# Causal scores of a linear-attention kernel: blocks of 32 keys on eight 64x32 tiles, second token half in reversed order of 32-blocks

## The chip, the cores and the metric

The kernel runs on one core of a Trainium2 chip (trn2). The metric is device time in microseconds (us), median of the runs. Before the change it is 446.14 us, with runs between 445.23 and 446.38.

## What is computed

For each of 16 sequences ("rows" of the kernel, B = 16) of T = 256 tokens and C = 128 channels, the kernel computes a layer norm, causal linear attention with 16 heads, a soft mixture of experts, and a residual. The change touches the attention only. Its part of the reference, cut:

```python
xn = layernorm(x)
q, k, v = split(xn @ Wqkv + bqkv)            # 16 heads of 8 channels
qf, kf = features(q), features(k)            # exp(clip(projection)), 64 values for each token and head
# causal linear attention, written as running sums:
kv_cur = cumsum(kf[:, f] * v[:, d]);  k_cur = cumsum(kf)
out = (qf . kv_cur) / max(qf . k_cur, 1e-6)
x = x + out @ Wout + bout + experts(xn)
```

The kernel evaluates the running sums as scores: S[key, query] = kf(key) . qf(query), masked so that a key counts only for queries at or after it, and then S times v.

## The kernel before

A row has 256 tokens in two halves of 128, one token to a partition. Within the second half the two blocks of 64 tokens stand in swapped order: partitions 0 to 63 hold tokens 0-63 and 192-255, partitions 64 to 127 hold tokens 64-127 and 128-191. `load_x` and `store` (L349 to L360) do this with two DMAs each.

Heads are worked in eight pairs p = 0 to 7. `project(b, g)` (L1093) makes the features of two pairs, `clip` on VectorE (L848) and `feature_exp` on ScalarE (L578) finish them in `feat`, where the two heads of a pair lie in partitions 0-63 and 64-127. `scores(b, p)` (L1109) forms the score blocks of both heads of one pair: for each of the four entries of `BLOCKS` (L30) and each head one f32 matmul of 64 contraction rows by 64 keys, with the queries streaming. An entry is (first key, first output partition, first query, last query, output column). The four entries stream 256, 192, 64 and 128 columns; entries one and three write partitions 0-63, two and four partitions 64-127, so each half of the output partitions gets 320 columns, and with two heads four 64x64 tiles of the array are in use. The output is `p_s` for even p and `p_t` for odd p, one PSUM bank for each head.

`evac_a` (VectorE, L854, with the mask `causal`) and `evac_b` (ScalarE, L584; the mask follows on GpSimd, L488) copy the scores to SBUF; `evac_pair` (ScalarE, L590, and L482) does both heads of pairs 6 and 7. `context` (L1127) multiplies them with v in 24 f32 matmuls on four 128x32 tiles, the line L1133. `causal` has 384 columns: 256 for keys of the first half, 128 for keys of the second.

The order on TensorE is written out by hand in `row` (L1356). Scores always come as two pairs one after the other, first on `p_s`, then on `p_t`; here each such couple is named by its pairs:

- logits of this row (L1070), scores 6 and 7 of the row before, transposed logits (L1211), context of heads of pairs 0 to 3 (L1133), shift (L1222, L1230), project 0 and 1 (L1105), slot sums (L1238), the next row's qkv product (L1070), slots transposed (L1246);
- scores 0 and 1, context of pairs 4 to 7 (L1133), scores 2 and 3;
- expert hidden layer (L1070), project 2 and 3, second expert layer (L1271, L1280) with transposes of the row before (L1175, L1181), combine (L1292), attention output (L1187), transposes of a later row (L1081);
- scores 4 and 5. Then the next row begins with its logits; rows 2 to 13 run in a hardware loop of two rows, with a branch at its end.

Before each call of `scores` the engine's sequencer waits for the exponentials (`fe_ok`) and for the bank to be free (`cl_ok` after the clip for pairs 0, 1, 4, 5; `ea_ok` and `eb_ok` after the evacuations for the others). The last entry of `BLOCKS` raises `sa_ok` and `sb_ok`, for which the evacuations wait.

Rows 0 and 15 are special: the first has its own prologue (weights are loaded, split and scaled, `causal` and `ident` are built on GpSimd from L428 on) and the last ends with a chain of small steps and the last store.

Of the kernel before, what the change touches and what calls it, by code (L numbers as in the profile page):

```python
# [13 lines left out]
B, T, C = 16, 256, 128  # L14
# [12 lines left out]
DEN_FLOOR = 1e-6  # L27
CLIP = 20.0
LOWEST = -3.0e38
BLOCKS = ((0, 0, 0, T, 0), (64, 64, 64, T, 64), (128, 0, 128, 192, 256), (192, 64, 128, T, 256))  # L30
LN_EXP = "natural_log_exp_and_others"
GELU = "gelu_and_others"
SQRT = "sqrt_and_others"
# [10 lines left out]
def landed(b, extra):  # L44

    i, u = b
    return i * 32 + 32 * extra

def after(eng, sem, value):  # L50
# [43 lines left out]
def build(nc, x, Wqkv, bqkv, Wout, bout, omega, nodes, weights, gamma_x, gamma_slot, slot_embeds,  # L94
          w1, w2, out):
    with ExitStack() as ctx:
        def sb(name, shape, dt=F32):
            return ctx.enter_context(nc.sbuf_tensor(name, shape, dt))
# [4 lines left out]
        def sem(name):  # L103
            return ctx.enter_context(nc.semaphore(name))
# [4 lines left out]
        causal = sb("causal", [128, 384])  # L109
# [34 lines left out]
        xin = sb("xin", [128, 2, TILES, C])  # L144
# [34 lines left out]
        out_sb = sb("out_sb", [128, 2, TILES, C])  # L179
# [129 lines left out]
        def heads_out(b):  # L309

            return p_t if is_row(b, B - 1) else x23

        def omega_part(t, r):

            return t[:, :, :].rearrange("p g (h r m) -> p (g h) r m", h=2, r=R)[:, :, r, :]
# [32 lines left out]
        def _(sp):  # L348
            def load_x(b, off):  # L349
                hold(sp, xg_ok, count(b, 1, -1))  # L350
                hold(sp, xr_ok, count(b, 1, -1))
                v = x[bass.ds(off, T), :].rearrange("(a p) c -> p a c", p=64)
                sp.dma_start(xin[0:64, b[1], :, :], v[:, 0:4:3, :]).then_inc(d_x[b[1]], 16)
                sp.dma_start(xin[64:128, b[1], :, :], v[:, 1:3, :]).then_inc(d_x[b[1]], 16)

            def store(b, off):
                hold(sp, o2_ok, count(b, 1, 1))
                v = out[bass.ds(off, T), :].rearrange("(a p) c -> p a c", p=64)
                sp.dma_start(v[:, 0:4:3, :], out_sb[0:64, b[1], :, :]).then_inc(d_out[b[1]], 16)
                sp.dma_start(v[:, 1:3, :], out_sb[64:128, b[1], :, :]).then_inc(d_out[b[1]], 16)  # L360

            def turn_stack(b):
                hold(sp, sthi_ok, count(b, 1, 1))
# [17 lines left out]
            first = x[0:T, :].rearrange("(a p) c -> p a c", p=64)  # L381
            sp.dma_start(xin[0:64, 0, :, :], first[:, 0:4:3, :]).then_inc(d_x[0], 16)
            for h in range(2):
                sp.dma_start(se_rows[:, 2 * h:2 * h + 2, :], slot_embeds[256 * h:256 * h + 256, :].rearrange(
                    "(c p) d -> p c d", p=128)).then_inc(d_se[h], 16)
# [12 lines left out]
            for u in range(2):  # L398
                o = 64 * u
# [4 lines left out]
            for u in range(2):  # L404
                o = 64 * u
# [10 lines left out]
            run_rows(sp, row)  # L416
            store((B // 2 - 1, 0), (B - 2) * T)
            sp.wait_ge(o2_ok, B)
            v = out[(B - 1) * T:B * T, :].rearrange("(a p) c -> p a c", p=64)
            sp.dma_start(v[:, 0:4:3, :], out_sb[0:64, 1, :, :]).then_inc(d_out[1], 16)  # L420
            for u in range(2):
                sp.wait_ge(d_out[u], 16 * B)

        LATE = 2

# [2 lines left out]
        def _(pool):  # L428
# [14 lines left out]
                                          fill=0.0, base=0, pattern=[[1, 128]], channel_multiplier=-1)  # L443
            last.then_inc(pool_id, 1)
            pool.wait_ge(pool_id, 4)
            pool.memset(causal[0:64, 320:384], 0.0).then_inc(pool_id, 1)
            pool.memset(causal[64:128, 256:320], 1.0).then_inc(pool_id, 1)
            pool.wait_ge(pool_id, 6)
            pool.tensor_scalar(neg_ident[:, :], ident[:, :], -1.0, None, ALU.mult).then_inc(pool_id, 1)
            pool.memset(xg[:, :, :, C:C + 1], 1.0)  # L450
            pool.memset(proc[:, :, C:C + 1], 1.0)
# [89 lines left out]
            v = s_sb[:, 6, 1, :].rearrange("p (a t) -> p a t", t=128)[:, 0:3:2, :]  # L541
# [5 lines left out]
        def _(act):  # L547
# [81 lines left out]
            first = x[0:T, :].rearrange("(a p) c -> p a c", p=64)  # L629
            act.dma_start(xin[64:128, 0, :, :], first[:, 1:3, :]).then_inc(d_x[0], 16)  # L630
# [133 lines left out]
            ctx_copy(last_row, 1)  # L764
            attn_copy(last_row)
            act.wait_ge(o2_ok, B)
            v = out[(B - 1) * T:B * T, :].rearrange("(a p) c -> p a c", p=64)
            act.dma_start(v[:, 1:3, :], out_sb[64:128, 1, :, :]).then_inc(d_out[1], 16)

        @block.vector
# [294 lines left out]
        def _(pe):  # L1066
# [42 lines left out]
            def scores(b, p):  # L1109
                after(pe, fe_ok, count(b, 4, p // 2 + 1))  # L1110
                if p in (0, 1, 4, 5):
                    hold(pe, cl_ok, count(b, 4, (1, 2, 0, 0, 3, 4)[p]))
                else:
                    hold(pe, ea_ok, count(b, 6, p - 1))
                    hold(pe, eb_ok, count(b, 6, p - 1))
                dst = (p_s, p_t)[p % 2]
                for keys, rows, lo, hi, o in BLOCKS:
                    for u, done in enumerate((sa_ok, sb_ok)):
                        f = feat[64 * u:64 * u + 64, p % 4, :]
                        mm = nc.tensor.matmul(dst[rows:rows + 64, u, o:o + hi - lo], f[:, T + keys:T + keys + 64],  # L1120
                                              f[:, lo:hi], start=True, stop=True, skip_group_check=True)
# [194 lines left out]
            pe.wait_ge(pool_id, 7)  # L1316

            def first_row():

# [118 lines left out]
```

## Time and profile before

| | before |
|---|---|
| median of three runs | 446.14 us (445.23 to 446.38) |
| the profiled execution | 445.07 us |
| its span, first to last instruction | 443.3 us |
| TensorE matmul busy | 431.2 us, 97% |
| VectorE busy | 347.5 us, 78% |
| ScalarE busy | 320.0 us, 72% |
| GpSimd busy | 186.3 us, 42% |
| granted TensorE clock | 0.999 of 2.4 GHz |

The page of the profile gives busy time of each engine, the span in 40 slices, and the chain of work that ended last. The trace behind it can be asked for groups of instructions (by line, tile and shape), for instructions in order of time in a stretch, and for what each engine waited for. PE is TensorE's matmuls, PEld its weight loads, DVE VectorE, ACT ScalarE, POOL GpSimd, SP SyncE; a q behind a name is the engine's sequencer or its DMA issue. An f32 matmul shows as two records of the same shape, so that a score of one pair (eight matmuls) is sixteen records.

### The profile page before, as it was taken

The page shows a single profiled execution, that of the slowest core. Times are in us where ns is not written, and L with a number is a line of the kernel's source. Part 1 is how long each engine was busy: PE and PEld are TensorE (multiplying, and loading weights), DVE is VectorE, ACT ScalarE, POOL GpSimd, SP SyncE. Part 2 cuts the span into 40 slices and gives each one's busy share as a digit, 9 for nine tenths or more (in the row PEclk, how much of TensorE's full clock was granted, in tenths as well). Part 3 has the DMA queues.
Part 4 walks back from the last instruction along what each step waited for, and adds up shares of the span by engine and source line. Part 5 has one row for each costly group of instructions (what it writes and reads, how often), then busy time and mean ns, then how long its engine had stood idle before and what let it go on. Part 6 is the DMA issues. An engine that isn't in the chain of part 4 may idle for free.

```text
span 443.3 us, 15786 instructions
## 1 busy us (share of the span) xinstructions
PE 431.2 (97%) x5726; PEld 361.1 (81%) x5726; DVE 347.5 (78%) x872; ACT 320.0 (72%) x533; POOL 186.3 (42%) x278
## 2 busy tenths in 40 slices
PE   6889999999999999999999999999999999999896
PEld 3568888888888889888888988888898888889785
DVE  7898777978878797878869787796978779576653
ACT  4767786858768686786868678586876859677681
POOL 5424444543435444343643443464345345434320
PEclk9999999999999999999999999999999999999999
DMA  4400321030202003020110302011030200203001
GB/s 93 107 25 3 62 49 27 1 63 14 53 20 47 18 6 59 12 47 24 37 23 12 59 12 47 24 22 37 12 59 12 47 12 9 51 1 61 2 1 25
DMA packets 45323, 14.37 MB, mean 32 GB/s; under 512 B 35376, under 2 KB 45168, under 8 KB 45296
## 3 DMA queue, kind: packets, MB, share of 16 engines
q1 hardware_dynamic: 44448, 13.48, 14.8%
q10 hardware_dynamic: 720, 0.53, 0.4%
q8 instruction: 17, 0.28, 0.3%
q0 software_dynamic: 128, 0.01, 0.1%
q14 instruction: 10, 0.08, 0.1%
HBM read 3.44 MB, written 2.10 MB: 12 GB/s over the span
## 4 chain that ended last, share of the span: by engine, by line
PE 93%; DVE 4%; ACT 2%; issue 1%; DVEq 0%; ACTq 0%
PE x L1070 20%; PE p_s L1120 10%; PE p_t L1120 8%; PE x L1271 7%; PE x L1238 7%; PE x L1280 6%; PE x L1292 6%; PE x L1133 5%; PE p_s L1133 5%; PE x L1211 4%; PE p_s L1105 2%; PE x L1222 2%; PE x L1246 2%; PE x L1187 2%; PE p_t L1105 2%; PE x L1175 1%
## 5 line engine op out<-in xcount | busy, mean ns | idle before, releaser
L488 POOL TENSOR_TENSOR s_sb<-s_sb,causal 128x256 f32<-128x256 f32 x96 | 68.3, 731 | 79.5 <-ACT s_sb L584 79.5
L578 ACT ACTIVATE feat<-arg,f_bias 128x1024 f32<-128x1024 f32 x64 | 71.8, 1147 | 8.4 <-DVE arg L848 8.3
L848 DVE TENSOR_SCALAR arg<-p_s,f_low,f_high 128x1024 f32<-128x1024 f32 x32 | 42.9, 1340 | 18.7 <-PE p_s L1105 12.2
L1120 PEld LDWEIGHTS p_s<-feat 64*64 64x64 f32 x1024 | 38.8, 132 | 17.2 <-issue 15.5
L1120 PE MATMUL p_s<-feat 64*64 64x256 f32 (+3 forms) x1024 | 49.5, 309 | 1.3 <-ACT feat L578 1.3
L329 POOL TENSOR_TENSOR qk_sq<-qkv 128x512 f32<-128x512 f32 x15 | 15.6, 1040 | 82.9 <-DVE qkv L825 82.9
L482 POOL TENSOR_TENSOR s_sb<-s_sb,causal 128x512 f32<-128x512 f32 x30 | 37.6, 1276 | 26.0 <-ACT s_sb L590 26.0
L1120 PE MATMUL p_t<-feat 64*64 64x256 f32 (+3 forms) x1024 | 47.1, 299 | 0.3 <-issue 0.3
L1120 PEld LDWEIGHTS p_t<-feat 64*64 64x64 f32 x1024 | 41.3, 133 | 1.8 <-issue 0.4
L848 DVE TENSOR_SCALAR arg<-p_t,f_low,f_high 128x1024 f32<-128x1024 f32 x32 | 42.7, 1335 | 0.0
L1238 PEld LDWEIGHTS x<-xg,disp 128*128 128x128 f32 x256 | 29.9, 191 | 8.2 <-ACT disp L606 8.2
L1271 PEld LDWEIGHTS x<-w_sb,hid_t 128*128 128x128 f32 x256 | 29.9, 191 | 7.1 <-ACT hid_t L618 6.6
L584 ACT ACTIVATE s_sb<-p_s 128x384 f32<-128x384 f32 x48 | 23.5, 490 | 15.8 <-PE p_s L1120 15.8
L889 DVE TENSOR_REDUCE maxima<-x 128x2 bf16<-128x512 f32 x32 | 20.6, 686 | 17.0 <-PE x L1211 17.0
L1238 PE MATMUL x<-xg,disp 128*128 128x129 f32 x256 | 33.0, 281 | 0.7 <-ACT disp L606 0.5
L1271 PE MATMUL x<-w_sb,hid_t 128*128 128x128 f32 x256 | 33.1, 282 | 0.1
L618 ACT ACTIVATE hid_t<-x 128x1024 f32<-128x1024 f32 x32 | 32.7, 1021 | 0.3
L590 ACT ACTIVATE s_sb<-p_s 128x768 f32<-128x768 f32 x15 | 12.2, 812 | 28.1 <-PE p_s L1120 28.1
L1292 PE MATMUL x<-proc,comb_t 128*128 128x129 f32 x256 | 31.5, 275 | 0.0
L1280 PE MATMUL x<-w_sb,hid_t 128*128 128x128 f32 x256 | 31.2, 275 | 0.0
L1292 PEld LDWEIGHTS x<-proc,comb_t 128*128 128x128 f32 x256 | 29.9, 191 | 0.2 <-issue 0.2
L1280 PEld LDWEIGHTS x<-w_sb,hid_t 128*128 128x128 f32 x256 | 29.8, 192 | 0.0
(165 smaller groups left out, 1035.4 us busy)
## 6 DMA issues: line engine op xcount, KB each, us to landing
xin<-in_L_attn_x_dram SPq DMA_DIRECT2D x31, 64.0 KB, 2.3
out_dram<-out_sb SPq DMA_DIRECT2D x31, 64.0 KB, 2.1
se_rows<-n_L_ffn_slot_embeds_dram SPq DMA_DIRECT2D x2, 128.0 KB, 4.4
w_f<-in_L_ffn_w_dram SPq DMA_DIRECT2D x1, 256.0 KB, 4.0
w_sb<-in_L_ffn_w_dram SPq DMA_DIRECT2D x1, 256.0 KB, 4.0
stack_t<-stack SPq DMA_TRANSPOSE x16, 4.3
wqkv_f<-in_L_attn_Wqkv_dram ACTq DMA_DIRECT2D x1, 192.0 KB, 4.1
bqkv_bc<-in_L_attn_bqkv_dram ACTq DMA_DIRECT2D x1, 192.0 KB, 4.8
```

Source lines behind the costliest of these rows:

```text
L482: pool.tensor_tensor(v, v, m, ALU.mult).then_inc(mb_ok, 1)
L488: pool.tensor_tensor(v, v, m, ALU.mult).then_inc(mb_ok, 1)
L578: nc.scalar.activation(feat[:, k:k + 2, :], arg[:, k:k + 2, :], ACT.Exp, bias=f_bias[:, 0:1]).then_inc(fe_ok, 1)
L618: nc.scalar.activation(hid_t[:, 2 * half:2 * half + 2, :], (x01, x23)[half][:, :, :], ACT.Gelu).then_inc(ge_ok, 1)
L848: nc.vector.tensor_scalar(arg[:, k:k + 2, :], (p_s, p_t)[g % 2][:, :, :], f_low[:, 0:1], f_high[:, 0:1], ALU.max, ALU.min).then_inc(cl_ok, 1)
L1070: mm = nc.tensor.matmul(dst, a, w, start=start and i == 0, stop=stop and i == 2, skip_group_check=True)
L1120: mm = nc.tensor.matmul(dst[rows:rows + 64, u, o:o + hi - lo], f[:, T + keys:T + keys + 64], f[:, lo:hi], start=True, stop=True, skip_grou ...
L1133: mm = nc.tensor.matmul(dst[32 * q:32 * q + 32, j, :], vw[:, b[1], kt, QUADS * a + q, :], s_sb[:, p, q % 2, o:o + 128], start=(kt == 0 and ...
L1238: mm = nc.tensor.matmul(x01[:, half, 129 * (c % 2):129 * (c % 2) + 129], disp[:, j, 128 * c:128 * c + 128], xg[:, b[1], j, :], start=(j == ...
L1271: nc.tensor.matmul(x01[:, c // 2, o:o + 128], hid_t[:, m, 128 * c:128 * c + 128], w2_sb[:, m, :], start=(m == 0 and c % 2 == 0), stop=Fals ...
L1280: mm = nc.tensor.matmul(x01[:, c // 2, o:o + 128], hid_t[:, m, 128 * c:128 * c + 128], w2_sb[:, m, :], start=False, stop=(m == 3), skip_gr ...
L1292: mm = nc.tensor.matmul(x23[:, 0, 129 * j:129 * j + 129], comb_t[:, c, 128 * j:128 * j + 128], proc[:, c, :], start=(c == 0 and j == 0), s ...
```

## The change

`BLOCKS` gets eight entries of 32 keys instead of four of 64. For keys k = 0, 32, 64, 96 of the first half the queries k to 255 stream (256, 224, 192 and 160 columns), written to output partitions k to k+31. The second half of the tokens is now stored in reversed order of its four blocks of 32: position block 4 holds tokens 224-255, block 7 holds tokens 128-159. There the block of keys at 128+k meets the positions 128 to 128+k+31: 32, 64, 96 and 128 columns. Each of the four groups of 32 output partitions gets 288 columns, and with two heads eight 64x32 tiles are in use. Loads and stores of a row take four DMAs of 32 partitions each, instead of two of 64; the mask is set with six small memsets instead of two; counts in semaphores follow. The first load and the last store are split between SyncE and ScalarE, two DMAs each instead of one.

```diff
-BLOCKS = ((0, 0, 0, T, 0), (64, 64, 64, T, 64), (128, 0, 128, 192, 256), (192, 64, 128, T, 256))
+KEYS = 32
+BLOCKS = (tuple((k, k, k, T, k) for k in range(0, 128, KEYS))
+          + tuple((128 + k, k, 128, 128 + k + KEYS, 256) for k in range(0, 128, KEYS)))
@@ landed
-    return i * 32 + 32 * extra
+    return i * 64 + 64 * extra
@@
+        def quarter(rows, q):
+
+            v = rows.rearrange("(a p) c -> p a c", p=32)
+            return v[:, q:8 - q:7 - 2 * q, :]
@@ load_x (store likewise, with out and out_sb)
-                v = x[bass.ds(off, T), :].rearrange("(a p) c -> p a c", p=64)
-                sp.dma_start(xin[0:64, b[1], :, :], v[:, 0:4:3, :]).then_inc(d_x[b[1]], 16)
-                sp.dma_start(xin[64:128, b[1], :, :], v[:, 1:3, :]).then_inc(d_x[b[1]], 16)
+                for q in range(4):
+                    sp.dma_start(xin[32 * q:32 * q + 32, b[1], :, :], quarter(x[bass.ds(off, T), :], q)
+                                 ).then_inc(d_x[b[1]], 16)
@@ first load on SyncE (ScalarE takes q = 2, 3), and the last store in the same way
-            sp.dma_start(xin[0:64, 0, :, :], first[:, 0:4:3, :]).then_inc(d_x[0], 16)
+            for q in range(2):
+                sp.dma_start(xin[32 * q:32 * q + 32, 0, :, :], quarter(x[0:T, :], q)).then_inc(d_x[0], 16)
@@ causal
-            pool.memset(causal[0:64, 320:384], 0.0).then_inc(pool_id, 1)
-            pool.memset(causal[64:128, 256:320], 1.0).then_inc(pool_id, 1)
-            pool.wait_ge(pool_id, 6)
+            for q in range(4):
+                if q > 0:
+                    pool.memset(causal[32 * q:32 * q + 32, 256:256 + 32 * q], 1.0).then_inc(pool_id, 1)
+                if q < 3:
+                    pool.memset(causal[32 * q:32 * q + 32, 288 + 32 * q:384], 0.0).then_inc(pool_id, 1)
+            pool.wait_ge(pool_id, 10)
@@ scores
-                        mm = nc.tensor.matmul(dst[rows:rows + 64, u, o:o + hi - lo], f[:, T + keys:T + keys + 64],
+                        mm = nc.tensor.matmul(dst[rows:rows + KEYS, u, o:o + hi - lo], f[:, T + keys:T + keys + KEYS],
                                               f[:, lo:hi], start=True, stop=True, skip_group_check=True)
-                        if keys == 192:
+                        if keys == T - KEYS:
                             mm.then_inc(done, 1)
```

## Rows read from the trace of the kernel before

**Rows 1.** The page: busy time and share of the span by engine; clock by slice.

```profile
PE 431.2 (97%) x5726; PEld 361.1 (81%) x5726; DVE 347.5 (78%) x872; ACT 320.0 (72%) x533; POOL 186.3 (42%) x278
...
PEclk9999999999999999999999999999999999999999
...
PE 93%; DVE 4%; ACT 2%; issue 1%; DVEq 0%; ACTq 0%
```

**Rows 2.** Windows of one row each: stretch, its length, busy time of each engine.

```profile
core 0: us, PE busy (x) PEld busy (x) DVE busy (x) ACT busy (x) POOL busy (x), PEclk, DMA share, GB/s
...
199.00:225.20 26.20, 26.20 (x358) 22.30 (x357) 21.41 (x54) 19.60 (x33) 11.59 (x17) 1.00 0.15 30
225.20:251.40 26.20, 26.16 (x358) 22.20 (x357) 21.26 (x54) 19.37 (x32) 11.32 (x17) 1.00 0.15 30
```

**Rows 3.** Groups by shape, stretch 211.55 to 212.9: xcount | busy us, mean ns.

```profile
L1120 PE MATMUL p_t<-feat 64*64 64x256 f32 x4 | 0.6, 377 | 0.0
...
L1120 PE MATMUL p_t<-feat 64*64 64x192 f32 x4 | 0.5, 322 | 0.0
...
L1120 PE MATMUL p_t<-feat 64*64 64x128 f32 x4 | 0.4, 269 | 0.0
...
L1120 PE MATMUL p_t<-feat 64*64 64x64 f32 x4 | 0.3, 217 | 0.0
```

**Rows 4.** Groups of weight loads by shape, stretch 210.1 to 213.0.

```profile
L1133 PEld LDWEIGHTS x<-s_sb,vw 128*32 128x32 f32 x48 | 1.2, 110 | 0.1
L1120 PEld LDWEIGHTS p_t<-feat 64*64 64x64 f32 x16 | 0.6, 134 | 0.0
```

**Rows 5.** Line L1120 in the 0.02 us from 211.60: engine op xcount: duration ns min/median/max.

```profile
L1120 PEld LDWEIGHTS p_s<-feat x3: 129/129/129, 211.6 to 211.6; 64*64 64x64 f32 x3
L1120 PE MATMUL p_s<-feat x3: 373/427/427, 211.6 to 211.6; 64*64 64x256 f32 x2, 64*64 64x192 f32 x1
```

**Rows 6.** Line L1120 on PE from 212.00 to 212.05: what is in flight.

```profile
L1120 PE MATMUL p_s<-feat x8: 269/350/427, 211.6 to 212.0; 64*64 64x256 f32 x4, 64*64 64x192 f32 x2, 64*64 64x128 f32 x2
```

**Rows 7.** PE in order of time: start us, us, what; scores 2 and 3.

```profile
210.15 1.52 PE L1133 MATMUL x<-s_sb,vw 128*32 128x128 f32 x48
211.60 0.77 PE L1120 MATMUL p_s<-feat 64*64 64x256 f32 x16
212.20 0.72 PE L1120 MATMUL p_t<-feat 64*64 64x256 f32 x16
212.85 0.50 PE L1070 MATMUL x<-slot_hi,w_hi 128*128 128x512 f32 x1
```

**Rows 8.** The same for scores 0 and 1 and the clip before them on DVE.

```profile
207.97 1.33 DVE L848 TENSOR_SCALAR arg<-p_t,f_low,f_high 128x1024 f32<-128x1024 f32 x1
...
208.80 0.77 PE L1120 MATMUL p_s<-feat 64*64 64x256 f32 x16
209.45 0.77 PE L1120 MATMUL p_t<-feat 64*64 64x256 f32 x16
```

**Rows 9.** ACT and PE in order of time, where the second expert layer begins.

```profile
213.94 1.28 ACT L735 ACT_TABLE_LOAD   x1
215.23 1.02 ACT L618 ACTIVATE hid_t<-x 128x1024 f32<-128x1024 f32 x1
...
216.38 2.05 PE L1271 MATMUL x<-w_sb,hid_t 128*128 128x128 f32 x16
```

**Rows 10.** DVE and PE in order of time at the end of a row.

```profile
223.78 0.42 DVE L816 TENSOR_TENSOR xt_lo<-x,xt_hi 128x256 fp32r<-128x256 f32 x1 [0.27 <-ACT xt_hi L561]
...
224.50 0.50 PE L1070 MATMUL x<-se_hi,xt_hi 128*128 128x512 f32 x1
```

**Rows 11.** Chain of waits, one piece: start us, us, what.

```profile
210.21 1.46 PE x L1133 x48
```

**Rows 12.** DMA issues of SyncE and ScalarE: start us, us; and the first norm on DVE.

```profile
0.82 0.74 SPq L382 DMA_DIRECT2D xin<-in_L_attn_x_dram  x1
4.01 2.88 SPq L324 DMA_DIRECT2D omega_f<-in_L_attn_omega_dram  x8
...
440.53 0.70 ACTq L768 DMA_DIRECT2D out_dram<-out_sb  x1
...
3.95 0.42 DVE L786 BATCH_NORM_STATS2 bn<-xin 128x6 f32<-128x128 f32 x2
```

**Rows 13.** Waits: who waited for whom, us in total, times, longest.

```profile
POOL xres L463 <- DMA bout_bc<-in_L_attn_bout_dram: 5.2, 1, 5.2
...
SPq L62 <- ACT stack L571: 166.4, 15, 16.9
```

More of the change, by code:

```diff
@@ L351, in load_x @@
                 hold(sp, xr_ok, count(b, 1, -1))
-                v = x[bass.ds(off, T), :].rearrange("(a p) c -> p a c", p=64)
-                sp.dma_start(xin[0:64, b[1], :, :], v[:, 0:4:3, :]).then_inc(d_x[b[1]], 16)
-                sp.dma_start(xin[64:128, b[1], :, :], v[:, 1:3, :]).then_inc(d_x[b[1]], 16)
+                for q in range(4):
+                    sp.dma_start(xin[32 * q:32 * q + 32, b[1], :, :], quarter(x[bass.ds(off, T), :], q)
+                                 ).then_inc(d_x[b[1]], 16)
             def store(b, off):
                 hold(sp, o2_ok, count(b, 1, 1))
-                v = out[bass.ds(off, T), :].rearrange("(a p) c -> p a c", p=64)
-                sp.dma_start(v[:, 0:4:3, :], out_sb[0:64, b[1], :, :]).then_inc(d_out[b[1]], 16)
-                sp.dma_start(v[:, 1:3, :], out_sb[64:128, b[1], :, :]).then_inc(d_out[b[1]], 16)
+                for q in range(4):
+                    sp.dma_start(quarter(out[bass.ds(off, T), :], q), out_sb[32 * q:32 * q + 32, b[1], :, :]
+                                 ).then_inc(d_out[b[1]], 16)
             def turn_stack(b):
@@ L379, in spread @@
                 return sp.dma_start(dst[:, :], src.rearrange("(a n) -> a n", a=1).broadcast_to([dst.shape[0], n]))
-            first = x[0:T, :].rearrange("(a p) c -> p a c", p=64)
-            sp.dma_start(xin[0:64, 0, :, :], first[:, 0:4:3, :]).then_inc(d_x[0], 16)
+            for q in range(2):
+                sp.dma_start(xin[32 * q:32 * q + 32, 0, :, :], quarter(x[0:T, :], q)).then_inc(d_x[0], 16)
             for h in range(2):
@@ L418, in _ @@
             sp.wait_ge(o2_ok, B)
-            v = out[(B - 1) * T:B * T, :].rearrange("(a p) c -> p a c", p=64)
-            sp.dma_start(v[:, 0:4:3, :], out_sb[0:64, 1, :, :]).then_inc(d_out[1], 16)
+            for q in range(2):
+                sp.dma_start(quarter(out[(B - 1) * T:B * T, :], q), out_sb[32 * q:32 * q + 32, 1, :, :]
+                             ).then_inc(d_out[1], 16)
             for u in range(2):
-                sp.wait_ge(d_out[u], 16 * B)
+                sp.wait_ge(d_out[u], 32 * B)
         LATE = 2
@@ L445, in _ @@
             pool.wait_ge(pool_id, 4)
-            pool.memset(causal[0:64, 320:384], 0.0).then_inc(pool_id, 1)
-            pool.memset(causal[64:128, 256:320], 1.0).then_inc(pool_id, 1)
-            pool.wait_ge(pool_id, 6)
+            for q in range(4):
+                if q > 0:
[3 more added lines that the diff above has]
+            pool.wait_ge(pool_id, 10)
             pool.tensor_scalar(neg_ident[:, :], ident[:, :], -1.0, None, ALU.mult).then_inc(pool_id, 1)
@@ L627, in spread @@
                 return act.dma_start(dst[:, :], src.rearrange("(a n) -> a n", a=1).broadcast_to([dst.shape[0], n]))
-            first = x[0:T, :].rearrange("(a p) c -> p a c", p=64)
-            act.dma_start(xin[64:128, 0, :, :], first[:, 1:3, :]).then_inc(d_x[0], 16)
+            for q in range(2, 4):
+                act.dma_start(xin[32 * q:32 * q + 32, 0, :, :], quarter(x[0:T, :], q)).then_inc(d_x[0], 16)
             spread(node_b, nodes, R).then_inc(d_feat, 16)
@@ L766, in _ @@
             act.wait_ge(o2_ok, B)
-            v = out[(B - 1) * T:B * T, :].rearrange("(a p) c -> p a c", p=64)
-            act.dma_start(v[:, 1:3, :], out_sb[64:128, 1, :, :]).then_inc(d_out[1], 16)
+            for q in range(2, 4):
+                act.dma_start(quarter(out[(B - 1) * T:B * T, :], q), out_sb[32 * q:32 * q + 32, 1, :, :]
+                              ).then_inc(d_out[1], 16)
         @block.vector
@@ L1315, in _ @@
             pe.wait_ge(vz_const, 2)
-            pe.wait_ge(pool_id, 7)
+            pe.wait_ge(pool_id, 11)
             def first_row():
```

## The prediction, made before the changed kernel was run

> **What bounds the kernel now.** I read the page first: TensorE matmuls are busy for 97% of the span, at full clock in all slices, and 93% of the chain that ended last is theirs [rows 1]. The question is whether other engines end some wait inside a row. The windows of single rows say no: of 26.20 us, TensorE is busy 26.20 and 26.16, while VectorE has 21.4 and ScalarE 19.6 [rows 2]. So a nanosecond saved on TensorE counts until another engine's line of work becomes the later one, and that I check at each place by instructions in order of time.
>
> **What a score costs now.** A row has four couples of scores, 64 in all over 16 rows. In scores 2 and 3 the first begins at 211.60, the second at 212.20, the next stage at 212.85: 1.25 us for a couple [rows 7]. By shape, 64 columns more take 322-269 = 53 ns, and 377-322 = 55: 0.83 ns for a column of a record [rows 3]. Each strip of 64 output partitions streams 320 columns in two records each: 2 x 320 x 0.83 = 531 ns. Two scores make 1.06 us of the 1.25; the remaining 0.19 are the first weight load that nothing hides, the staggered start, and the drain and change of tile shape at the end, about 0.2 between the last context matmul and the first score as well. So the score is bound by columns, not by instructions: the loads after the first are hidden.
>
> **The change, part by part.**
>
> Columns: 288 in place of 320, 2 x 288 x 0.83 = 478 ns, 53 less for a score, 106 for a couple [rows 3].
>
> The unhidden first load: 32 columns wide instead of 64. Loads of the two widths take 110 and 134 ns as records, so 24 less, once a couple [rows 4]. The staggered start: three of the four tiles begin within 0.02 us, some 6.7 ns apart [rows 5]; eight tiles need four steps more, +27 ns, once a couple. The two cancel.
>
> Sixteen matmuls in place of eight for a score, 32 records instead of 16. No row shows what eight tiles do together; the trace has four 64x64 tiles and four 128x32 tiles. From below, the cost is nothing: tiles start apart by 6.7 ns [rows 5], 32 of them are 214 ns of a score's 478. I exclude a gain. From above, the only long run of narrow tiles is the context, 48 records in 1.46 us, 30 ns each [rows 11]; 32 x 30 = 973 ns for a score. I take nothing, since 128 columns on four tiles need 4 x 0.83 x 128 / 4 = 106 ns for a round of four, 27 ns each, so that the context too is bound by its columns and not by its count.
>
> Work order inside a score: matmuls of different tiles pass one another. At 212.00 to 212.05 the 128-column records are in flight while no 64-column record is, although these stand before them in the list [rows 6]. The new lists need this over a longer stretch. I take it that each tile is served by itself; what happens if not is a rival below.
>
> Now where the 0.10 us of each couple goes. Scores 0 and 1: the second can't begin before its bank is clipped. The clip ends at 207.97+1.33 = 209.30 and the score begins at 209.45 [rows 8], 0.65 after the first instead of 0.60. Here only the second score gains: 0.05. Scores 2 and 3: 0.10. Both stand on a stretch whose other line (clip, qkv bias, norms on VectorE, then square root, evacuation, table load and GELU on ScalarE) contains no score that it waits for long. It ends at 215.23+1.02 = 216.25, and TensorE takes it at 216.38 [rows 9]. With about 0.05 for the hand-over TensorE can be earlier by 0.1 at most, so the two couples together bring 0.10, not 0.15. Scores 4 and 5: the low half of the transposed rows ends at 223.78+0.42 = 224.20, the logits begin at 224.50 [rows 10]; 0.10 fits. In the six loop ends the branch and the waits of the next row stand behind twice as many instructions in TensorE's sequencer; the trace doesn't show its lead, so between 0.10 gained and 0.10 lost, and I take nothing gained there. Scores 6 and 7: 0.10.
>
> A row gives 0.30, or 0.20 at a loop end: 9 x 0.30 + 6 x 0.20 = 3.9 us. Row 0 waits for others for much of its time and counts as nothing.
>
> DMAs. In the loop, SyncE issues four more a row, each at most 0.74 us [rows 12]; it waits 166 us for ScalarE's stacks [rows 13], and the transpose queued behind has more slack than that. Nothing. At the start, the second halves are issued behind the first ones: 0.36 us for each of the small omega issues, 0.74 for the full one [rows 12], so about 0.5 later. The first norm begins at 3.95, after a memset, so most of it is hidden: +0.1, between 0 and +0.5, as every later load moves back too. At the end nothing hides the second issue on either queue: +0.5, between 0.36 and 0.7 [rows 12]. The four more memsets on GpSimd lie ahead of a wait of 5.2 us for a DMA [rows 13]: nothing; without that cover they would cost under 1 us once.
>
> Sum: -3.9 + 0.1 + 0.5 = -3.3 us. The profiled execution took 445.07 us (span 443.3) and would take 441.8. It lies 1.1 us under the median of 446.14; against the median the forecast is 442.8 us. About 0.3% (1.3 us) is what a measurement can tell from no change.
>
> **Rivals.**
>
> (1) Slower, because the work let into the array is bounded in program order. Before, a score has eight matmuls, two for each tile, and all eight may be in flight. Suppose eight is what fits, and that the ninth enters when the first is done. The first is now also the longest: 256 columns, 2 x 213 + 27 for its load = 0.45 us. The 160-column tile is done after 2 x 133 + 27 = 0.29 and stands idle; its 128-column matmul then runs from 0.47 to 0.71, and the second score ends at 1.25 in the same way. With the drain, a couple takes 1.34 instead of 1.25: +0.09 x 64 = 5.8 us, and with the ends +0.6, less what scores 0 and 1 hide behind the clip, 451.5 us, between 448 and 454. It decides as soon as fewer than some twelve matmuls fit. For it: nothing in the trace has more than two matmuls waiting on one tile. Against it: the passing seen in rows 6, which it allows too.
>
> (2) No change: the gain of the stream is given back between the two scores of a couple. There the sequencer takes two or three waits before it may send the next sixteen matmuls. Today this hides behind 0.6 us of stream; with twice the instructions ahead and a shorter stream, a gap of up to 0.1 in scores 2-3, 4-5 and 6-7 takes all of it: 446 us, between 444.8 and 447.3.
>
> (3) Far slower: a floor on record starts of 30 ns, the context's rate [rows 11]. A score takes 32 x 30 = 0.97, a couple 2.04 with its 0.1 of drain instead of 1.25: +0.79 x 64 = 50 us, 496 us. Against it are the three starts in 0.02 us [rows 5] and the reckoning of the context's columns above. The Trainium skill speaks for a rule of this kind: "TensorEngine Tiling (Array Packing)", section Instruction Overhead, puts about 60 cycles on each matmul and advises against taking the tiling factor from a dimension that is already small, and "TensorE: Matmul & The Clock Gate", section Back-to-back issue gap, states a floor near 25 ns between starts. By that figure a score would be an estimated 0.8 us and the kernel some 28 us slower, 474 us; the starts in rows 5 disagree for different tiles.
>
> **How the numbers follow.** Forecast (column bound, 442.8) 0.52, own range 441.0 to 444.8: all 64 couples at 0.10 with nothing at the start would even be 440.2, the sequencer bounds against it give 445. Rival 1 0.27, rival 2 0.13, rival 3 0.08. The range 441.0 to 453.5 leaves out rival 3 and the outer ends of the others. Faster by over 0.3%: 0.52. Within: 0.12. Slower: 0.36.
>
> **What would show it.** Right: score couples of 1.15 us from first score to next stage, p_s to p_t about 0.55 (0.65 in scores 0 and 1), rows of 25.9 to 26.0 us. Rival 1: records of the 128-column blocks start 0.45 or later after the score's first instead of 0.3, couples of 1.3. Rival 2: first records of p_t start late, behind an idle stretch put down to issue. Rival 3: starts evenly spaced by 25 to 30 ns. The prediction is wrong at the root if the change of shape costs more with eight tiles than the 0.2 us seen, or if the evacuations start late because the last block ends last.

## The result, and the profile after

| | before | after |
|---|---|---|
| median of four runs each, on the same chip | 445.98 us (445.23 to 446.38) | 474.75 us (474.07 to 475.83) |
| span of the profiled execution | 443.3 us | 473.2 us |
| TensorE matmul busy | 431.2 us | 443.9 us |
| mean granted TensorE clock | 0.999 | 0.982 |

The changed kernel takes 1.066 times as long, with a 95% interval of 1.0645 to 1.0677. That is slower by 28.8 us, where the forecast was 3.3 us faster. It also lies far above the range of 441.0 to 453.5.

Lines of the page of after: those that correspond to [rows 1], between them the queue that carries code, and last the logits as a group of instructions:

```profile
PE 443.9 (94%) x7774; PEld 367.8 (78%) x7774; DVE 345.8 (73%) x872; ACT 320.4 (68%) x533; POOL 187.2 (40%) x282
...
PEclk9999999999899998999989999899998999999999
...
q8 instruction: 68, 1.11, 1.0%
...
PE 89%; issue 5%; DVE 4%; ACT 1%; ACTq 0%; DVEq 0%
...
L1082 PE MATMUL x<-se_hi,xt_hi 128*128 128x512 f32 x32 | 14.2, 443 | 18.2 <-issue 17.5
```

Four things differ from before. TensorE's share of the chain fell from 93% to 89%, and "issue", time in which nothing that the profile shows was waited for, rose from 1% to 5%. The clock row has five dips at equal distances. The queue that carries code (kind "instruction") moved 68 packets of 16 KB. In the page of before the same line reads:

```profile
q8 instruction: 17, 0.28, 0.3%
```

And of 18.2 us of idle time ahead of the logits, 17.5 are "issue": the logits open a row, and right before them stands the branch of the loop.

The windows around the first turn of the loop in after (stretch, its length, busy time by engine, granted clock, DMA share, GB/s):

```profile
119.00:121.00 2.00, 2.00 (x71) 1.64 (x69) 1.62 (x6) 1.56 (x3) 0.00 (x0) 1.00 0.00 0
121.00:124.00 3.00, 0.05 (x4) 0.00 (x0) 0.84 (x2) 0.54 (x2) 1.41 (x2) 1.00 0.12 28
124.00:126.00 2.00, 1.64 (x6) 1.05 (x6) 0.64 (x2) 0.00 (x0) 0.00 (x0) 0.89 0.17 39
126.00:129.00 3.00, 3.00 (x68) 2.49 (x68) 0.76 (x4) 1.10 (x2) 0.32 (x1) 0.51 0.00 0
129.00:132.00 3.00, 3.00 (x67) 2.56 (x66) 2.44 (x8) 1.13 (x3) 2.89 (x3) 1.00 0.02 5
```

From 121 to 124 all engines run dry; then TensorE works on, at first at full clock, and from 125.6 for 3.4 us at half. What it does at the turn itself is one line of the loop's own instructions, first in after, then in before (duration in ns, min/median/max; PEldq is TensorE's sequencer):

```profile
L89 PEldq COMPARE_BRANCH  x6: 82/3425/3832, 120.6 to 410.1; - x6
```

```profile
L87 PEldq COMPARE_BRANCH  x6: 76/210/251, 119.4 to 380.5; - x6
```

The branch is met six times and taken five times (the shortest, 82 and 76 ns, is the last one, which falls through). Taken, it costs 0.21 us before and 3.3 to 3.8 us after. From the start of one scores 4-5 to the next, a row without the turn takes 26.39 us in after and one with it 31.3 to 31.8: 4.9 to 5.4 us a turn, 25.6 us of the 29.9 by which the span grew.

The rest is inside the rows. PE in order of time in after, scores 6-7, read as in [rows 7]:

```profile
211.73 0.72 PE L1132 MATMUL p_s<-feat 64*32 64x256 f32 x32
212.25 0.91 PE L1132 MATMUL p_t<-feat 64*32 64x256 f32 x32
213.09 0.33 PE L1223 MATMUL x<-ident,log_sb 128*128 128x128 f32 x1
```

The first score takes 0.52, a little less than the 0.55 of the forecast, but the second takes 0.84: the couple 1.35 instead of 1.25. All four couples of a row read 1.35 at full clock, where before only scores 0 and 1 did, behind the clip [rows 8]; 3 x 0.10 a row are some 5 us. So there are two losses, and the experiments take them one by one.

### The profile page after: what moved, and what is told of

Its sections match the earlier page's. It is cut to its first block, busy times and chain, and to the rows that moved or that the text cites. A ratio compares the mean times of both kernels' runs of the same rounds, so it can differ in the third digit from the quotient of the medians.

```text
span 473.2 us, 20052 instructions
## 1 busy us (share of the span) xinstructions
PE 443.9 (94%) x7774; PEld 367.8 (78%) x7774; DVE 345.8 (73%) x872; ACT 320.4 (68%) x533; POOL 187.2 (40%) x282
## 3 DMA queue, kind: packets, MB, share of 16 engines
q8 instruction: 68, 1.11, 1.0%
## 4 chain that ended last, share of the span: by engine, by line
PE 89%; issue 5%; DVE 4%; ACT 1%; ACTq 0%; DVEq 0%
PE x L1082 19%; PE p_t L1132 10%; PE p_s L1132 9%; PE x L1283 7%; PE x L1250 7%; PE x L1292 6%; PE x L1304 6%; PE p_s L1145 5%; PE x L1145 5%; PE x L1223 4%; PE p_s L1117 2%; PE x L1234 2%; PE x L1258 2%; PE x L1199 1%; PE p_t L1117 1%
## 5 line engine op out<-in xcount | busy, mean ns | idle before, releaser
L1132 PE MATMUL p_t<-feat 64*32 64x32 f32 (+7 forms) x2048 | 58.4, 300 | 0.3 <-issue 0.3
L1132 PEld LDWEIGHTS p_s<-feat 64*32 64x32 f32 x2048 | 37.5, 110 | 18.7 <-issue 16.8
L1132 PE MATMUL p_s<-feat 64*32 64x256 f32 (+7 forms) x2048 | 48.6, 301 | 1.5 <-ACT feat L589 1.3
L1132 PEld LDWEIGHTS p_t<-feat 64*32 64x32 f32 x2048 | 45.7, 110 | 2.3 <-issue 0.4
L894 DVE TENSOR_SCALAR_CACHE_REDUCE log_sb<-x 128x512 f32<-128x512 f32 x32 | 22.1, 691 | 21.6 <-PE x L1082 21.4
L1250 PEld LDWEIGHTS x<-xg,disp 128*128 128x128 f32 x256 | 29.9, 191 | 8.1 <-ACT disp L617 8.1
L1283 PEld LDWEIGHTS x<-w_sb,hid_t 128*128 128x128 f32 x256 | 29.9, 191 | 7.1 <-ACT hid_t L629 6.6
L1082 PE MATMUL x<-se_hi,xt_hi 128*128 128x512 f32 x32 | 14.2, 443 | 18.2 <-issue 17.5
```

Source lines behind the costliest of these rows:

```text
L1082: mm = nc.tensor.matmul(dst, a, w, start=start and i == 0, stop=stop and i == 2, skip_group_check=True)
L1132: mm = nc.tensor.matmul(dst[rows:rows + KEYS, u, o:o + hi - lo], f[:, T + keys:T + keys + KEYS], f[:, lo:hi], start=True, stop=True, skip_ ...
L1250: mm = nc.tensor.matmul(x01[:, half, 129 * (c % 2):129 * (c % 2) + 129], disp[:, j, 128 * c:128 * c + 128], xg[:, b[1], j, :], start=(j == ...
L1283: nc.tensor.matmul(x01[:, c // 2, o:o + 128], hid_t[:, m, 128 * c:128 * c + 128], w2_sb[:, m, :], start=(m == 0 and c % 2 == 0), stop=Fals ...
```

## The experiments

### The loop written out, in both kernels

```diff
-    with eng.Fori(1, B // 2 - 1) as i:
+    for i in range(1, B // 2 - 1):
         for u in range(2):
             row((i, u), False, True, True)
```

> The changed kernel with rows 2 to 13 written out instead of a hardware loop (no branch on any engine; nothing else differs). Theory A (the branch at the loop's end must wait for TensorE's code to be loaded again, since a body of 2037 instructions is no longer held; five turns of some 4.8 us with the half-clock stretch behind each): the five stalls go, the 16 KB code transfers stay but lie beside the work, full clock throughout, 474.7 - 24 = 450.5 us, with couples still at 1.35. Rival B (the stall belongs to a wait or a transfer at the end of the second row, with four loads and four stores a row on SyncE): stalls of 3 us stay at the ends of rows 3, 5, 7, 9, 11, and the time stays at 470 to 475 us.

> The kernel before, written out in the same way, as control. Theory A: its branch takes 0.21 us behind a full queue and no code is loaded in its loop, so nothing is to be gained: 446 us, ratio 0.998 to 1.002. If written-out code had a price of its own (code streaming in all the time), this shows it, and the other run is to be read against this one.

Measured: the changed kernel written out 451.16 us (450.19 to 451.39), ratio to before 1.012 (1.0102 to 1.0139); the kernel before written out 444.83 us, ratio 0.9988 (0.9979 to 0.9998). The five stalls and all clock dips are gone, though now more code is streamed in than in the kernel before. The page of the changed kernel written out:

```profile
PE 436.6 (97%) x7774; PEld 362.5 (81%) x7774; DVE 345.5 (77%) x872; ACT 320.8 (71%) x533; POOL 187.1 (42%) x282
...
PEclk9999999999999999999999999999999999999999
...
q8 instruction: 62, 1.02, 0.9%
...
PE 93%; DVE 4%; ACT 1%; issue 1%; DVEq 0%; ACTq 0%
```

So writing out takes away 474.75 - 451.16 = 23.6 us, and rival B falls: waits, DMAs and matmuls are the same in both. That is a little less than the 25.6 us of the five turns, because three rows of the written-out kernel are 0.3 to 0.5 us longer than the others, 1.3 us in all; the kernel before, written out, has no such row. What is left, 451.16 - 444.83 = 6.3 us, are mostly the couples: a row takes 26.39 us against 26.02, and the 15 rows from the first scores on give 15 x 0.37 = 5.6. In the profiled executions, whose spans are 6.8 us apart, the rest are those three rows, less 0.2 us at the end of the kernel.

### Token order and DMAs without the small blocks

```diff
-BLOCKS = (eight entries of 32 keys)
+WIDE = ((64, 0, 0, 0, T, 0), (64, 64, 64, 64, T, 64), (64, 128, 0, 128, 192, 256), (64, 192, 64, 128, T, 256))
```

> The changed kernel (reversed order of 32-blocks in memory, four loads and stores a row, its mask and memsets), but with scores again in four blocks of 64 keys on 64x64 tiles, which this token order allows too. Theory: everything lost lies in the 32-key matmuls and their number; order and DMAs cost at most the first load and last store, 446.1 to 447 us, couples 1.25, no stall at the loop's end. Rival B: the stalls stay, 465 us or more.

Measured: 444.86 us (444.73 to 445.66), ratio 0.9986 (0.9977 to 0.9996); couples 1.25, 17 code packets. Nothing of the loss lies in the order of tokens, in the doubled DMAs, or in the mask. The time even lies under the 446.1 us from which I expected it, and 0.5 us under the 445.38 of the kernel before; 0.2 us of that are the end of the kernel (below).

### How large the loop's body may be

The records of TensorE's instructions from one branch to the next are 1525 before and 2037 after: 16 scores an iteration with eight f32 matmuls more each, and four records (two loads, two matmuls) for each. A kernel with eight different lists had 1925 and stalled too. Two kernels in between use 64-key blocks in some couples, 32-key blocks in the others, in the better order that is found below:

```diff
+    if 4 * b[1] + p // 2 not in (1, 2, 6):        # five_couples: (1, 2, 3, 5, 6)
+        return both(WIDE)
+    return both((SECOND + FIRST, FIRST + SECOND)[p % 2])
```

> Loop kept; the 32-key blocks (short first, then long first) only in scores 2-3 and 4-5 of even rows and 4-5 of odd rows, the last ones right before the branch; elsewhere 64-key blocks. Loop body 1717 instructions instead of 1525 (before: branch 0.21 us, no code loaded) and 2037 (changed: branch 3.3 to 3.8 us, nine 16 KB transfers a turn). Theory A1 (what counts is how many 16 KB blocks of 256 instructions the body spans; room for seven of them besides the one loaded ahead, so that the limit is near 1792): branch 0.2 us, no transfers. Theory A2 (eight-tile matmuls right before the branch bring the stall): branch over 3 us.

> The same with five of eight couples, body 1845 instructions; the look at eight lists had 1925 and stalled (3.5 to 3.9 us). Theory A1 with room for seven blocks: it stalls, over 3 us and eight or nine transfers a turn. With room for eight blocks and a favourable start of the body it may not; then the limit lies between 1845 and 1925.

Measured, one run each: 445.28 us with three couples, 472.89 with five. The branch in the first, the branch in the second, and the second's clock:

```profile
L103 PEldq COMPARE_BRANCH  x6: 76/208/234, 119.5 to 381.0; - x6
```

```profile
L103 PEldq COMPARE_BRANCH  x6: 83/3688/3848, 120.2 to 408.9; - x6
```

```profile
PEclk9999999999899998999979999799997999999999
```

Theory A2 falls, for the kernel with three couples has eight-tile matmuls right before its branch; A1 holds. Up to 1717 records the code stays with the engine from turn to turn; at 1845 nine transfers of 16 KB come in every turn, as in after, and the whole gain of a shorter stream is gone many times over. A turn costs even more here, 5.6 to 6.6 us, and in three of the five the clock stays at half for 6.8 us instead of 3.4. A later kernel had 1781 and didn't stall, so the limit lies between 1781 and 1845 records. That kernel and the one with five couples have the same number of TensorE instructions in all (7006 matmul records each), so the length of the whole program isn't what decides. The Trainium skill has the rule, which I had not weighed: "Runtime: NRT & Kernel Launch", section Instruction fetch mechanics, gives TensorE room for 2048 instructions, filled in blocks of 256, and says that a taken branch whose target is outside the current window of two pages stalls for a fetch. The traces agree with the stall and with blocks of 16 KB (68 packets, 1.11 MB). They differ in two points: a body of up to 1781 records, about seven such blocks, was kept whole and didn't stall, and the limit met here is lower than 2048 by 200 to 270 records.

The kernel with three couples shows a small loss too, at every turn, at which 1.0 us instead of 0.65 pass from p_t to the logits:

```profile
223.19 0.72 PE L1147 MATMUL p_s<-feat 64*32 64x32 f32 x32
223.71 0.72 PE L1147 MATMUL p_t<-feat 64*32 64x256 f32 x32
224.69 0.49 PE L1096 MATMUL x<-se_hi,xt_hi 128*128 128x512 f32 x1 [0.26 <-issue]
```

The branch and the next row's waits come after p_t's 64 instructions, and p_t is over before the sequencer is through with them. In the changed kernel it can't be told apart from the stall.

### Why the second score of a couple is late

In after, the first score's 128-column blocks are under way at 0.34 us, while the 256-column ones still run (TensorE, stretch 212.06 to 212.085; 18 records in flight or begun, the shortest, 269 ns, of 128 columns):

```profile
L1132 PE MATMUL p_s<-feat x18: 269/347/400, 211.7 to 212.1; 64*32 64x256 f32 x4, 64*32 64x224 f32 x4, 64*32 64x192 f32 x4, 64*32 64x160 f32 x4
```

So passing works, as in [rows 6], and rival 1 in its stated form, a window of eight, is out. But of the second score only one record has begun by 0.63 us after the first score's start; the next starts 135 ns after it, and then all follow 16.7 ns apart (stretch 212.25 to 212.37):

```profile
L1132 PE MATMUL p_t<-feat x1: 379/379/379, 212.2 to 212.2; 64*32 64x256 f32 x1
```

Two kernels with up to eight different lists of blocks each were to tell what this depends on; the list was chosen by couple and parity of the row. The second of them is written out and leaves some blocks out.

> Eight lists of blocks in one kernel, one for each couple and parity of row; the output is the same. Read: each couple's time from first score to next stage. Even rows: scores 0-1 the list of the changed kernel (control, 1.35), 2-3 all blocks of one head and then of the other, 4-5 both halves of the list reversed (160, 192, 224, 256, then 128, 96, 64, 32 columns), 6-7 the four short blocks first. Odd rows: 0-1 four 64-key blocks (control, 1.25 or 1.35 behind the clip), 2-3 the 256-column block cut in two (18 matmuls a score), 4-5 two 64-key blocks and four of 32, 6-7 four of 32 and two of 64. In the changed kernel the second score's first matmul starts in time, its second one only 92 ns after the last of the first score has streamed, as after a change of tile shape. Theory C (a score fills a limit of 16 matmuls, and what comes behind waits until all is done): any list of 16 keeps 1.35; the matmul that is late is the second with 16, and an earlier one with 18 (the last of the first score itself); lists of 12 have no such wait, unless the change between 64x64 and 64x32 tiles drains by itself. Theory D (the wait is between particular tiles, by place and order): the list by heads or the reversed one comes to 1.15 to 1.25.

> Written out, eight cases again. Two of them leave work out: scores 4-5 of even rows lack the 32-column block (14 matmuls a score), scores 2-3 of odd rows the 32- and the 64-column block (12 a score), otherwise in the order of the changed kernel. Theory W (16 places, freed in order): the late matmul of the second score is its second one with 16 a score (seen), so the fourth one with 14 and the sixth with 12; those before it start in time. Theory T (a drain before the second matmul on eight tiles, whatever the number): it is the second one in all three. Of the orders of 16: short first, then long first (scores 0-1 and 2-3 of even rows) 1.15 to 1.20 by theory W, 0-1 not under 1.2 as the clip gates it; long first, then short first (6-7 even) 1.3 or more; the same with all lists reversed (0-1 odd) 1.2; reversed long-then-short and then the changed kernel's order (4-5 odd) 1.25 to 1.3; short first in both (6-7 odd) 1.26 as in the look before.

Measured, one run each: 493.83 us for the first, which has the loop and its stalls (1925 records), and 447.16 us for the second. The couples from first score to next stage (PE in order of time; rows behind a turn or with a gap put down to issue are left out, but for the last line):

| list, first score then second | columns in the order sent | couple, us |
|---|---|---|
| as changed | 256, 224, 192, 160, 32, 64, 96, 128, both scores | 1.353 |
| one head, then the other | the same | 1.43 to 1.68 |
| reversed | 160, 192, 224, 256, 128, 96, 64, 32, both | 1.30 |
| reversed, then as changed | | 1.29 |
| long first, then short first | | 1.353 |
| as changed, 14 matmuls; 12 matmuls | less the 32; less the 32 and 64 | 1.32; 1.29 |
| short first | 32, 64, 96, 128, 256, 224, 192, 160, both | 1.26 |
| short first, then long first | | 1.170, 1.26 behind the clip |
| the same, all lists reversed | | 1.26 behind the clip |
| 64-key blocks | | 1.248, 1.35 behind the clip |
| 64-key and 32-key blocks in one score | | 1.86 to 1.97 |
| 18 matmuls a score | | 1.38 and 1.39 in the rows outside the loop; 1.82 to 2.61 in it |

The decisive rows are the two lists that leave work out. With 14 matmuls a score, the second score's third one begins in time and its fourth is late; with 12, the fifth begins in time and the sixth is late. The records of p_t that have begun by 0.64 us, with 14 (three, from three matmuls; the fourth begins at 0.65), and with 12 (seven: five matmuls, and the second records of two; the sixth begins at 0.65):

```profile
L1155 PE MATMUL p_t<-feat x3: 349/376/376, 92.9 to 93.0; 64*32 64x256 f32 x2, 64*32 64x224 f32 x1
```

```profile
L1155 PE MATMUL p_t<-feat x7: 323/349/376, 160.7 to 160.9; 64*32 64x224 f32 x4, 64*32 64x256 f32 x2, 64*32 64x192 f32 x1
```

16 + 1, 14 + 3, 12 + 5: it is always the 18th matmul from the start of the couple that is late. Theory T falls and W holds: TensorE has room for 16 f32 matmuls. The 17th gets its place when the oldest is done (in the changed kernel the 256-column one, at 0.45 us by the reckoning of the prediction), and the 18th, after this standstill, much later, although the two oldest start, and so end, only 7 ns apart: in after the weights of the 17th begin to load at 0.49 us and those of the 18th at 0.65, 160 ns behind. The list with 18 matmuls a score shows it within one score: its 17th begins at 0.35 us and its 18th, of the same shape on another tile, at 0.44, where the last two of a list of 16 begin 7 ns apart, at 0.34. That costs the couple some 0.03 us. In the loop the same couples are longer: the second score begins 0.1 us later and then has a stretch of 0.1 to 0.9 us in which no matmul starts. The cause of that is open. Where the oldest eight are the short blocks, it is the 10th matmul of the second score that is late (at 0.72 us, 1.26 in all). Where the short ones are the oldest in the first score and the long ones come first in the second, the late places fall where long blocks stream, and nothing is idle. Why the second place comes so late, no run tells; nor whether the room is counted in matmuls or in instructions, as every matmul of a score is f32. The Trainium skill gives TensorE a queue of 64 ("Advanced Engine Details and Errata", section Engine Queue Depths: 64, complicated with tiling); with four instructions for an f32 matmul the 16 seen here are the same number.

Of the expectations for the first kernel, both theories fell as they were worded. Theory C wanted 1.35 for every list of 16, and the reversed one took 1.30 and the one with short blocks first 1.26; theory D wanted 1.15 to 1.25 for the list by heads or the reversed one. Theory W is C with one thing changed: a place is given back when the oldest is done, and not when all are. Its expectations for the second kernel held, but for the reversed twin of the best list behind the clip, which took 1.26 where I expected 1.2. That blocks of both sizes in one score cost 0.6 to 0.7 us a couple more was expected only as a possibility: at every change between 64x64 and 64x32 tiles the array is emptied, and the next record begins 93 ns after the last column of the other shape (reckoned with 0.83 ns a column).

### The better order

```diff
+    return both((SECOND + FIRST, FIRST + SECOND)[p % 2])
```

> The changed kernel written out (451.2 us), with one thing more: the first score of each couple lists its short second-half blocks first (32, 64, 96, 128, then 256, 224, 192, 160 columns), the second score the long ones first (256, 224, 192, 160, then 32, 64, 96, 128). Theory W (TensorE takes 16 f32 matmuls ahead, 64 instructions, and gives a place back only when the oldest of them is done; in the changed kernel the oldest is the 256-column one, done at 0.45 us, and from standstill the second place comes some 155 ns after the first): with this order the first score's oldest eight are done by 0.32 us, so the second score's eight long ones are in time, and its short ones are sent while the long ones stream. Couples 1.15 to 1.20 instead of 1.35, 64 of them less what the clip and the GELU line hold back: 438 to 443 us. Theory T (a drain between scores on eight tiles, whatever the order): couples stay at 1.26 to 1.35, 447 to 451 us.

Measured: 443.71 us (443.43 to 445.24), ratio 0.996 (0.9947 to 0.9974): 7.4 us faster than the same kernel in the old order. The two ran on different chips, on which the kernel before took 445.57 and 445.38 us. Its couples, and how many records of p_t have begun by 0.64 us (eight, where the old order has one):

```profile
211.45 0.72 PE L1145 MATMUL p_s<-feat 64*32 64x32 f32 x32
211.97 0.72 PE L1145 MATMUL p_t<-feat 64*32 64x256 f32 x32
212.62 0.50 PE L1094 MATMUL x<-slot_hi,w_hi 128*128 128x512 f32 x1
```

```profile
L1145 PE MATMUL p_t<-feat x8: 296/335/376, 212.0 to 212.0; 64*32 64x256 f32 x2, 64*32 64x224 f32 x2, 64*32 64x192 f32 x2, 64*32 64x160 f32 x2
```

The couple takes 1.17 us: nearly the column reckoning of the prediction (1.15), now that the matmuls come in time, and theory T falls. But the time lies 0.7 us above the 438 to 443 that I expected, for two reasons. A row takes 25.84 us against 26.02 in the kernel before written out: 0.18 less, not 0.30. A little is lost because a couple gains 0.08 us and not 0.10; most of the loss is at one place, the second expert layer. In the kernel before written out, and then in this one:

```profile
214.55 1.03 ACT L618 ACTIVATE hid_t<-x 128x1024 f32<-128x1024 f32 x1
215.66 0.52 PEld L1271 LDWEIGHTS x<-w_sb,hid_t 128*128 128x128 f32 x4 [0.42 <-ACT hid_t L618]
```

```profile
215.18 1.02 ACT L641 ACTIVATE hid_t<-x 128x1024 f32<-128x1024 f32 x1
216.26 0.86 PEld L1296 LDWEIGHTS x<-w_sb,hid_t 128*128 128x128 f32 x7 [0.52 <-ACT hid_t L641]
```

Counted from the start of scores 6-7 of the row before, TensorE is 0.20 earlier at the expert layer's first product and 0.10 earlier at the second: the weight loads' wait for GELU grows from 0.42 to 0.52 us.

The second reason: written out, five rows have a gap and are 0.2 to 1.1 us longer than the others, 2.7 us in all in the profiled execution, which at 445.24 us was the slowest of the five. A transfer of code lies within a few us of each gap, but one of 16 KB comes every 7 us, so that these traces don't show that the transfers make the gaps. One of the largest, inside a score:

```profile
237.81 0.60 PE L1145 MATMUL p_t<-feat 64*32 64x256 f32 x14
239.01 0.65 PE L1145 MATMUL p_t<-feat 64*32 64x160 f32 x18 [0.60 <-issue]
```

### A version inside the limit, and one with less code

> Loop kept; in it the 32-key blocks (short first, then long first) in four of the eight couples: scores 2-3, 4-5 and 6-7 of even rows and 2-3 of odd rows; the others, among them those right before the branch, with 64-key blocks. The four rows outside the loop have 32-key blocks everywhere. Without stall: four couples of 1.17 instead of 1.25, 6 x 0.32 = 1.9 us and some 1.2 in the rows outside, so 442.5 to 444.5 us; with stalls 466 or more.

> The fastest so far (written out, short first then long first, 443.7 us), but with 64-key blocks in scores 0 and 1, where the second score waits for the clip. 64 instructions a row less to load. In the written-out kernel stretches of 0.2 to 1.0 us appear in which TensorE has nothing to do right beside a code transfer, in some rows and not in others (about 3 us in all). If they come from the rate at which code is used, they become fewer with fewer instructions; against that stand the 0.09 us by which this couple is shorter. Fewer stalls win: 441 to 443.5 us; otherwise 444 to 445 us.

Measured: 443.21 us (442.53 to 443.81), ratio 0.9948 (0.9932 to 0.9964), for the loop with four couples; 443.23 us (442.39 to 445.09), ratio 0.9951 (0.9934 to 0.9968), for the written-out one with 64-key blocks at the clip. In the first, the branch is that of the kernel before, and none of its 22 code transfers lies between the first turn and the last:

```profile
L103 PEldq COMPARE_BRANCH  x6: 76/208/239, 119.1 to 378.6; - x6
```

```profile
q8 instruction: 22, 0.36, 0.3%
```

From its second turn on two of its rows take 51.90 us, without gaps, where two rows in the loop of the kernel before take 52.22: the 0.32 that was expected. The second still has gaps, 0.1 to 0.5 us of idle time at four places. Both beat the kernel before by half a per cent; they can't be told from one another, nor for certain from the 443.71 above, so that fewer instructions aren't shown to bring fewer gaps.

## Why the prediction was wrong, step by step

**What bounds the kernel, and the columns: right.** TensorE was the bound; 288 columns take nearly the forecast time. The first score lasts 0.52 us, and in the better order a couple lasts 1.17 where 1.15 was forecast: a gain of 0.08 and not 0.10.

**Sixteen matmuls for nothing: right for the stream, wrong for the queue.** In the first score the first records start 6.7 ns apart as in [rows 5], and the upper bound by the context's rate never applied. What failed is that I compared the count with the rate of starting only. With two matmuls for a tile and eight tiles one score fills all 16 places, so nothing of the second can be there early, and the first to leave is the longest. The size: +0.10 a couple instead of -0.10 (+0.05 behind the clip), 0.37 us a row, some 5.6 of the 6.3 us between the two written-out kernels; between the two orders it is 7.4 us. That the cause is the room and not the number of matmuls is shown by the better order, which has the same matmuls on the same tiles.

**The loop's end: the step that failed most.** It said that the branch stands behind twice as many instructions, "between 0.10 gained and 0.10 lost". I had weighed the sequencer's lead and not where its code comes from. The trace of before had the evidence: its 17 packets of code come up to 121 us, about the loop's first turn, and again from 387 us, after its last, none in between, so that the body was being kept, in a room that must end somewhere. To add a third to its instructions, from 1525 to 2037, was the question to ask. Writing the loop out gave 23.6 us back; the five turns read 25.6 us in the trace. Nor are there six such turns, as the text had it, but five.

**Where the gain goes in a row.** The bound by the GELU line was right in kind and value (0.10, [rows 9]), but applied too narrowly: it holds for all that comes before it in the row, the couple 6-7 too. With the 0.08 of scores 4-5 behind it that makes 0.18 a row, not 0.30. Even without both losses the kernel would have gained at most 16 x 0.18 = 2.9 us of the 3.9, an estimate from the rows of the written-out kernels.

**DMAs.** The four additional ones a row cost nothing, as forecast. Start and end were forecast at +0.6 and gave -0.2: the first norm begins at 3.95 as before, and from the last result to the end of the span pass 473.2 - 470.61 = 2.6 us instead of 443.3 - 440.50 = 2.8. All ten traces of kernels with the doubled DMAs show 2.61 to 2.63, both without them 2.82 and 2.83. I had counted the second issue and not that the DMAs, half as large, land sooner: 1.7 us from issue to landing instead of 2.3 (the last result and the last store's row in the list of DMAs, after and then before).

```profile
470.19 0.42 DVE out_sb L933
...
out_dram<-out_sb ACTq DMA_DIRECT2D x2, 32.0 KB, 1.7
```

```profile
440.07 0.43 DVE out_sb L921
...
out_dram<-out_sb ACTq DMA_DIRECT2D x1, 64.0 KB, 2.3
```

**The rivals.** Rival 1 named the right price, 1.34 for a couple, and the right kind of cause, room bounded in program order with the longest block the oldest, but the wrong number, eight. Of its tell-tales, the 128-column records not before 0.45 didn't appear (0.34), while the couples of 1.3 did. Rival 2's gap between the two scores didn't appear: the first record of p_t is in time. An idle stretch of its kind is real only at the branch (0.26 us with three couples). Rival 3's own sum, 496 us, is out. Beside it stands an estimate of 474 us by the floor near 25 ns between starts that the Trainium skill states ("TensorE: Matmul & The Clock Gate", section Back-to-back issue gap), and 474.75 was measured, but that is chance: starts on different tiles are 6.7 ns apart in after too, and 23.6 us of the difference vanish when the loop is written out. A total that fits says nothing of its cause. No rival held the code loading, and so the range could not reach it.

## What to carry to other kernels

Before adding instructions to a loop body, count them for each engine and look at the code queue (q8) in the page: if it is silent inside the loop, the body is being kept, and here 1781 records on TensorE were kept while 1845 cost 5.6 to 6.6 us in every turn. Where many small tiles run side by side, the order of the list is part of the cost: put short blocks where they will be the oldest when the next group has to enter, and stay with one tile shape. When one line of work has already capped the gain at a place in the row, add up everything that comes before it, not only its neighbours.

## What the runs showed of the hardware

- TensorE's taken branch: 0.21 us where no code was loaded in the loop, 3.3 to 3.9 us where it was. All engines run dry behind it, and the granted clock goes to half, 1.2 GHz, soon after TensorE works again, for 3.4 us in after (for 6.8 in three of five turns with 1845 records), so that a turn costs 4.9 to 5.4 us in after and not 3.3.
- 16 f32 matmuls (64 recorded loads and matmuls) are what TensorE took ahead over all tiles together: the 18th was late with 16, 14 and 12 in a score. Matmuls on different tiles pass one another (128 columns at 0.34 us, while 256-column ones ran), but a place is given back in program order, and after a standstill the second of them loaded its weights 160 ns after the first.
- After such a standstill the f32 matmuls of the second score started 16.7 ns apart, at full clock and at half clock (the couple at 126.2 us of after) alike; where they had been taken ahead they started 6.7 ns apart.
- Between 64x64 and 64x32 tiles the array is emptied, 93 ns from the last column to the next record: a first score made of both takes 0.93 or 0.96 us, one of 64x64 tiles alone 0.60, one of 64x32 tiles alone 0.52.
